# Group norms' statistics and coefficients kept in SBUF, with the openings of four stages rewritten

## The reference

```python
def _gn(v, G=32, eps=1e-5):
    B_, C_, H_, W_ = v.shape
    g = v.reshape(B_, G, C_ // G, H_, W_)
    m = jnp.mean(g, axis=(2, 3, 4), keepdims=True)
    s = jnp.var(g, axis=(2, 3, 4), keepdims=True)
    return ((g - m) / jnp.sqrt(s + eps)).reshape(v.shape)

x = x + _L0_conv_ref(_gn(x), ...)   # attention in a 5x5 window, 8 heads
x = x + _L1_conv_ref(_gn(x), ...)   # qkv, 5x5 depthwise + grouped 1x1, linear attention, projection
x = x + _L2_conv_ref(_gn(x), ...)   # per-channel softmax over a 7x7 window
x = x + _L3_conv_ref(_gn(x), ...)   # 3x3 convolution, its weights mixed per image from pooled _gn(x)
```

## Time and profile before

| | us |
|---|---|
| median of 3 runs | 7782.99 (7781.92 to 7786.57) |
| the profiled execution | 7781.12, span 7779.3 |
| PE busy | 7307.5 (94%) |
| DVE busy | 5660.4 (73%) |
| POOL busy | 4676.4 (60%) |
| ACT busy | 3664.9 (47%) |

### The profile page before, as it was taken

The page is one execution under the profiler, slowest core; times in us unless marked ns, Lnnn a source line. Parts: engine busy times, 40 slices in busy tenths (PEclk is TensorE's granted clock), DMA queues, the critical chain, the costliest instruction groups (busy, mean ns, idle before and its releaser), DMA issues. The chain is left out here.

```text
span 7779.3 us, 137220 instructions
## 1 busy us (share of the span) xinstructions
PE 7307.5 (94%) x53058; PEld 6275.6 (81%) x53058; DVE 5660.4 (73%) x8853; ACT 3664.9 (47%) x7040; POOL 4676.4 (60%) x2130
## 2 busy tenths in 40 slices
PE   5999998989998899699999999999999999997999
PEld 4777776879998777378888888888888888886999
DVE  5666666334443455499999999999999999996664
ACT  3565555423332333155555555555555555554322
POOL 3555553023333000189898899889898898895332
PEclk9999999999999999899999999999999999998999
DMA  3111112865555975122222222222222222214552
GB/s 140 66 62 59 59 62 73 298 179 147 148 145 144 259 210 167 58 53 59 64 51 51 64 63 53 55 60 53 60 63 59 49 57 65 60 41 117 151 161 78
DMA packets 651429, 751.13 MB, mean 97 GB/s; under 512 B 467573, under 2 KB 500469, under 8 KB 629222
## 3 DMA queue, kind: packets, MB, share of 16 engines
q1 hardware_dynamic: 581318, 483.44, 22.4%
q0 software_dynamic: 52288, 230.92, 12.1%
q10 hardware_dynamic: 17376, 30.54, 1.1%
HBM read 397.01 MB, written 193.76 MB: 76 GB/s over the span
## 5 line engine op out<-in xcount | busy, mean ns | idle before, releaser
L1960 POOL TENSOR_TENSOR e_ev<-e_se,e_v 128x1536 f32<-128x1536 f32 (+1 forms) x832 | 3073.9, 3822 | 242.5 <-ACT e_se L1891 242.0
L1891 ACT ACTIVATE e_se<-e_stage 128x512 f32<-128x512 f32 x2880 | 1714.7, 597 | 1517.2 <-PE e_stage L1707 1486.9
L2061 DVE SCALAR_TENSOR_TENSOR e_stage<-e_k,e_rl,e_qp 128x512 f32<-128x512 f32 x3136 | 2255.1, 745 | 223.7 <-ACT e_se L1891 184.6
L1714 PE MATMUL e_pv_sum<-e_ident,e_ev 128*128 128x128 f32 x12544 | 1821.9, 272 | 0.0
L1707 PE MATMUL e_stage<-e_top,e_minus 128*128 128x512 f32 x3136 | 1568.2, 502 | 101.3 <-DVE e_stage L2061 100.9
L1714 PEld LDWEIGHTS e_pv_sum<-e_ident,e_ev 128*128 128x128 f32 x12544 | 1480.9, 140 | 135.6 <-issue 85.2
L1714 PE MATMUL e_pe_sum<-e_ident,e_se 128*128 128x128 f32 x9472 | 1417.1, 272 | 12.8 <-ACT e_se L1891 12.8
L1714 PEld LDWEIGHTS e_pe_sum<-e_ident,e_se 128*128 128x128 f32 x9472 | 1173.6, 140 | 232.8 <-issue 40.1
L911 POOL DMA_DIRECT2D agg<-c_ot x384 | 334.9, 874 | 878.2 <-ACT c_ot L989 768.7
L403 POOL TENSOR_TENSOR a_pr<-a_pr,a_rden 128x480 f32<-128x480 f32 x512 | 495.0, 989 | 546.8 <-DVE a_rden L636 546.8
L1707 PEld LDWEIGHTS e_stage<-e_top,e_minus 128*128 128x128 f32 x3136 | 594.6, 190 | 233.3 <-DVE e_stage L2061 154.7
(11 more groups left out here) (180 smaller groups left out, 12371.1 us busy)
## 6 DMA issues: line engine op xcount, KB each, us to landing
e_acc<-e_se POOLq DMA_DIRECT2D x128, 1024.0 KB, 7.6
qkv<-b_ot SPq DMA_DIRECT2D x120, 512.0 KB, 5.9
c_xt<-qkv SPq DMA_DIRECT2D x384, 160.0 KB, 3.8
agg<-c_ot POOLq DMA_DIRECT2D x384, 160.0 KB, 2.5
f_ws<-in_L_w_sets SPq DMA_DIRECT2D x32, 1152.0 KB, 8.0
a_xb<-in_x SPq DMA_DIRECT2D x24, 768.0 KB, 5.0
a_xr<-in_x SPq DMA_DIRECT2D x32, 512.0 KB, 3.8
x<-a_xr SPq DMA_DIRECT2D x32, 512.0 KB, 2.7
```

Source lines behind the costliest of these rows:

```text
L1714: last = nc.tensor.matmul(total[:, c * PART:(c + 1) * PART], lhsT=src[:, c * PART:(c + 1) * PART], rhs=ident[:], is_transpose=True, start= ...
L1891: nc.scalar.activation(exps(t, j), stage[:, bank_of(t, j), :], ACT.Exp).then_inc(exp_done, 1)
L1960: nc.gpsimd.tensor_tensor(split(ev[(t * NG2 + g) % NEV][:, 0:size]), split(exps(t, o * K2 + i, size)), window(v[h], h, u, o, i, size), ALU ...
L2061: nc.vector.scalar_tensor_tensor(rows(stage[:, bank_of(t, j), :]), win, rl[:, h, o:o + 1], rows(qp[:]), ALU.add, ALU.mult).then_inc(multip ...
```

## The change

The statistics `st`, the coefficients `cf`, the pooled `mean` and the matrix `gm` become SBUF tiles of one object that lives through all blocks. The blocks `s_` and `n_` are gone: the chain of norm operations is the first thing that DVE, PE and ACT do inside the block that uses the norm, and nothing of it goes through DRAM. The measuring of the input is in `a_`, with three buffers in place of four, and the weights of `a_` are loaded between the maps. Then four openings are changed:

- `a_`: bands and masks of the first two bands are asked for while the maps are measured; from the third band on the coefficients are copied by a DMA from SBUF to SBUF.
- `c_`: only the first four groups' weights are loaded ahead of the first two groups of qkv, the rest behind them.
- `d_`: POOL's first two loads of the residual wait for the first turned tile.
- `e_`: the first band waits for its own tile to be cleared alone, the order of the clearing is changed, the upper edge of the first band isn't normalised and so needs no overwriting, the dummy products read weights and no longer x, and the first running extreme is opened ahead of the copies of V. For each band, statistics are written where they stay; the DMAs of coefficients and statistics are gone.
- `f_`: pairing the columns of the first two bands moves from DVE to POOL, the first weight set is asked for ahead of the first band, and ACT rounds the second band after the first weights.

The core of the diff:

```diff
-    norm_coefficients(nc, norm_sems, 2, stats[2], coef[2], w["group_mean"])
-    channel_attention(nc, norm_sems, xs[2], coef[2], xs[3], stats[3], ...)
+    channel_attention(nc, norm, xs[2], xs[3], w["L2_w_t"], w["L2_rel"], w["identity"], w["zeros"])
...
+    def product(self, pe, call, bank):
+        if call == 0:
+            pe.wait_ge(self.matrix_in, 16)
+        pe.wait_ge(self.averaged, call + 1)
+        self.nc.tensor.matmul(bank[:, 0:self.NS * 2], lhsT=self.gm[:], rhs=self.ms[:].rearrange("p n s -> p (n s)"),
+                              start=True, stop=True).then_inc(self.grouped, 1)
+    def root(self, act, call):
+        act.wait_ge(self.var_ready, call + 1)
+        self.nc.scalar.activation(self.std[:], self.var[:], ACT.Sqrt).then_inc(self.std_ready, 1)
+    def links(self, dve, call, bank, measured, pooled=False):
+        dve.wait_ge(self.measured, measured)
+        for i in range(self.NS):
+            h, b = divmod(i, B)
+            last = nc.vector.bn_aggr(ms[:, i, :], self.st[:, h, b])
...  (the chain that follows is that of L142 to L159)
 window_attention, sync
+            for k in range(0, NMAP, 2):
+                load_map(sp, k)
             sp.dma_start(wt[:], w_qkv_t.rearrange("(h p) o -> p h o", p=PART)).then_inc(consts_in, 16)
+            norm.load_matrix(sp)
...
+            for k in range(NMAP + NMAP % 2, B * HALVES, 2):
+                load_map(sp, k)
...
-                sp.dma_start(cf[u][:], coef[b]).then_inc(band_in[u], 16)
+                if g >= 2:
+                    sp.dma_start(cf[u][:], norm.cf[:, b]).then_inc(cf_in[u], 16)
 grouped_conv, sync
-            half = GROUPS // 2
-            for i in range(2):
-                sp.dma_start(band[:, i * half:(i + 1) * half], w_band[:, i * half:(i + 1) * half]).then_inc(consts_in, 16)
+            sp.dma_start(band[:, 0:EARLY], w_band[:, 0:EARLY]).then_inc(consts_in, 16)
             sp.wait_ge(border_zero, 2)
-            with sp.Fori(0, TURNS) as n:
+            load_groups(0)
+            half = (GROUPS - EARLY) // 2
+            for i in range(2):
+                part = slice(EARLY + i * half, EARLY + (i + 1) * half)
+                sp.dma_start(band[:, part], w_band[:, part]).then_inc(bands_in, 16)
+            with sp.Fori(1, TURNS) as n:
+                load_groups(n)
 linear_attention, gpsimd
+            pool.wait_ge(turned, 1)
             load(0)
 channel_attention
-            sp.wait_ge(cleared, CLEARED["e"])
+            sp.wait_ge(cleared, CLEARED["a"] + 1)
             load_band(0)
...
-            clear_edge(0)
...
-                nc.tensor.matmul(stage[:, i, :], lhsT=ident[:], rhs=xb[:, 0, 0:TPX], start=True, stop=True)\
+                nc.tensor.matmul(stage[:, i, :], lhsT=ident[:], rhs=wt[:, 0].rearrange("p h o -> p (h o)"), start=True, stop=True)\
...
+            normalise(0)
             act.wait_ge(cleared, CLEARED["e"])
-            normalise(0)
             for p in parts(0):
+                if p == "V0":
+                    open_extreme(0, OPENS[0])
                 copy_projection(0, p)
...
-            for x in (xb, *k, *v, near, pair):
+            for x in (xb, k[0], pair, near, v[0], k[1], v[1]):
 dynamic_conv, sync
+            load_set(0, 0)
             sp.wait_ge(cleared, CLEARED["f"])
             load_band(0)
-            for c in range(NWS):
+            for c in range(1, NWS):
 dynamic_conv, gpsimd
+            def pair_columns(u):
+                pool.wait_ge(normalised, (u + 1) * HALVES)
+                nc.gpsimd.tensor_tensor(to_pairs(u, 0, 2), of_columns(u, 0, 2), of_columns(u, 2, 2), ALU.subtract).then_inc(x_paired, 1)
+                nc.gpsimd.tensor_tensor(to_pairs(u, 2), of_columns(u, 1), of_columns(u, 2), ALU.add).then_inc(x_paired, 1)
+                nc.gpsimd.tensor_tensor(to_pairs(u, 3), of_columns(u, 2), of_columns(u, 1), ALU.subtract).then_inc(x_paired, 1)
+            pair_columns(0)
+            pool.wait_ge(paired, NPAIRED)
             for g in range(NG):
...
+                if g == 1:
+                    pair_columns(1)
                 pool.wait_ge(x_high_ready, g + 1)
 dynamic_conv, scalar
             round_x(0)
-            round_x(1)
             begin_mix(0, 1)
             round_w(0, 0)
+            round_x(1)
 dynamic_conv, vector
-            pair_columns(0)
-            mix(0, 0, 1)
-            pair_columns(1)
-            for k in range(2, K3):
+            for k in range(1, K3):
                 mix(0, 0, k)
```

More of the change, by code:

```diff
@@ L237, in window_attention @@
         consts_in = sem("consts_in")
-        cleared = sems["cleared"]
+        map_in = [sem(f"map_in{i}") for i in range(NMAP)]
+        cleared = norm.cleared
+        cf_in = [sem(f"cf_in{u}") for u in range(2)]
         normalised_x = sem("normalised_x")
@@ L554, in _ @@
         def _(act):
+            for k in range(1, B * HALVES, 2):
+                load_map(act, k)
             act.wait_ge(consts_in, 64)
@@ L623, in _, with measure_map @@
         def _(dve):
+            def measure_map(k):
+                b, h = divmod(k, HALVES)
+                dve.wait_ge(map_in[k % NMAP], (k // NMAP + 1) * 16)
+                for i in range(STATS):
+                    last = nc.vector.bn_stats(norm.st[:, h, b, i, :], xm[k % NMAP][:, i * NPX // STATS:(i + 1) * NPX // STATS])
+                last.then_inc(norm.measured, 1)
+            for k in range(B * HALVES):
+                measure_map(k)
+            norm.links(dve, 0, pj, MEASURED["a"])
             dve.wait_ge(consts_in, 64)
@@ L702, with qkv_project @@
 CROWS = CHUNK // WW
-def qkv_project(nc, x_in, coef, qkv, w_t):
+def qkv_project(nc, norm, x_in, qkv, w_t):
     ctx = ExitStack()
@@ L777, in _ @@
         def _(pe):
+            norm.product(pe, 1, pq[:, 0])
             pe.wait_ge(w_low_ready, 1)
@@ L1392, with channel_attention @@
 NG2 = K2 * len(ROW_PARTS)
[L1395 removed]
+def channel_attention(nc, norm, x_in, x_out, w_t, rel, ident_in, zeros):
     ctx = ExitStack()
@@ L1801, in _ @@
         def _(act):
+            norm.root(act, 2)
             act.wait_ge(consts_in, 80)
@@ L2146, with dynamic_conv @@
 COLUMN_ORDER = (0, 2, 1)
-def dynamic_conv(nc, sems, x_in, coef, pooled, x_out, w1_t, w2_t, b2, w_sets, ident_in):
+def dynamic_conv(nc, norm, x_in, x_out, w1_t, w2_t, b2, w_sets, ident_in):
     ctx = ExitStack()
```

317 lines of the change are left out of this document (134 added, 183 removed).

## The result

The changed kernel takes **7691.29 us** (median of 4 runs, 7678.91 to 7693.47), beside 7782.45 (7779.42 to 7786.57) for the kernel before on the same chip; ratio 0.9879, 95% interval 0.9862 to 0.9896. The forecast was 7696, 7682 to 7716. The profiled execution spans 7690.6 us: 88.7 less than before, where the sum of terms said 87.0.

The account below looks back on a forecast made before the run. PE was taken to bound the kernel, busy 94% of the span, with idle time to win in the openings. Terms summed to -87.0 us from 7781.1, giving 7694.1; the median's 1.9 more made 7696, range 7682 to 7716.

Parts of the forecast that it names:

- `a_`, term -16.1: Opening of `a_`: PE's first product comes 16.1 us earlier (13.4 to 17.3), with the last map 0.8 late.
- each map landing about 1 us before its turn, except the last: Measuring in `a_`: with three buffers every map but the last arrives about 1 us before DVE needs it.
- `f_`, first weights, -16.0: Opening of `f_`: the first turned weights on PE come 16.0 us earlier.
- DVE's first mix waits until about 7130, and all after it slips by 1.4: Opening of `f_`: POOL's pairing holds DVE's first mix until about 7130, making all after it 1.4 us later.
- `f_`, second weight, +0.5: Mixes of `f_`'s second weight: POOL's pairing and rest of band 1 meet DVE again, costing 0.5 us.
- Behind the first convolution, which has 13 us: `f_`, second weight: POOL's 11 to 13 us meeting DVE lie behind the first convolution's 13 us, so 0.5 is left.
- Rival 1: Blocked and shared: last map half-shared +2.7, PE cold in projections +1.7, POOL and DVE holding in `f_` +5.5; 7706, chance 0.17.
- Loops, 0: Loops: DMAs of coefficients and statistics go or become copies inside SBUF; nobody waited for them, so 0 us.
- `d_`, 0: Opening of `d_`: bound by bytes, so moving 1 MB to 10 us later gives 0 us (-3 to +2).
- gains given back: Gains of `c_` and `f_` lost to later weights, sets and bands by DMA; 7720 us, chance 0.05.
- copies in `a_`'s loop: SBUF copies of coefficients delay each of 30 bands in `a_`; with 5 us a band 7846 us, chance 0.03.
- old DMAs: A stage's chain could still wait for an old DMA; near no change, the rest of the chances, 0.01.

Follow-up runs that it names:

- kept_warm: Changed kernel with dummy PE products in `a_`, `c_`, `e_`, `a_`'s constants behind the maps, `d_`'s residual later, `f_`'s band 1 paired by DVE; 7693.29 us.
- other_orders: Changed kernel with `a_`'s maps split over two queues, two groups' weights ahead in `c_`, `e_` awaiting all clears, `f_`'s first set behind the band; 7696.30 us.
- parts_undone: Changed kernel with one part undone each: `c_` weights first, `d_` residual at once, `e_` extreme behind V, `f_` columns paired by DVE; 7708.81 us.
- all_openings: openings_further plus dummy PE products in `a_`, 11 of them as soon as the constants are there; 7668.05 us.
- before_padded: Kernel before with only an unused tile of 2272 bytes a partition ahead of all others; 7775.50 us.
- norms_alone: Changed kernel with the redrawn openings of `c_`, `d_`, `e_`, `f_` undone, except `e_`'s upper edge, dummy products and clearing order; 7717.53 us.
- before_cf_first: Kernel before with `cf` allocated ahead of all other tiles of `f_`, moving the weights by 64 bytes; 7772.01 us.
- changed_again: The changed kernel itself, unaltered, run again for a second trace of the same program; 7686.28 us.
- openings_further: Changed kernel with maps over both queues in `a_`, dummy products in `c_` and `e_`, `f_`'s first set behind the band and adds moved earlier; 7682.39 us.

## Why the prediction was right, step by step

The time was right (the forecast lay 4.7 us above the median), and the mechanisms of `b_`, `c_` and `e_` hold with their sizes: -10.2 for -10.5, -8.4 for -9.0, -29.8 for -31.0 (the band flew 8.8 us where I took 7.6), -3.6 to -6.7 by the pairs of traces for -4.9 inside `e_`. But the sum hides errors of both signs, and that they cancel is luck.

- **`a_`, term -16.1:** -10.5 to -15.4 by the pairs of traces, -12.7 by the means; 1.0 of the difference is in the base, since the trace that the forecast was worked out from has 81.2 where the mean of three is 80.2. The failing step is "each map landing about 1 us before its turn, except the last": DVE waited 1.34 us for the sixth map in one trace and 2.09, 1.29 and 1.07 for three maps in the other, and the first came at 14.5. Maps that fly side by side are what makes it late: with the constants behind the maps it still came at 14.1 (kept_warm), with one map after the other at 9.7 (other_orders). What kept single maps back is not shown.
- **`f_`, first weights, -16.0:** -17.4. The step "DVE's first mix waits until about 7130, and all after it slips by 1.4" failed: POOL's three pairings took 4.8 us, not 5.6 and more, and were over at 7059.57, when DVE's first mix became free to start anyway (7059.41). Hold: 0.14 us for my 1.4.
- **`f_`, second weight, +0.5:** +4.0. "Behind the first convolution, which has 13 us" was the wrong cover: the first adds are queued on DVE behind these mixes, and PE waits for them. parts_undone sets the pairing's whole worth at 0.7 to 1.5 us. Rival 1 named this mechanism and put 5.5 on it. Its other two parts didn't come in the first trace; in the second, the first projection of `a_` was 4.1 behind the forecast's 65.1, by late maps, and the opening of `e_` 1.3 longer than forecast, by the clock.
- **Loops, 0:** `f_` is 6 us shorter, by where its tiles stand, which no part of the argument looked at; `e_` 1.0 to 2.9, cause not sought.
- **`d_`, 0:** neither confirmed nor refuted. By the means the opening is 1 us shorter, but the rate of its DMAs moves it by up to 8 with nothing changed, more than the edit could.

By the means of the table, the gain is 3.4 us smaller in `a_`, 2.1 in the opening of `f_`, 2.1 over `b_`, `c_` and `e_`, and 8 larger in the loops of `e_` and `f_`. The loop of `e_` stayed within 5 us; by more than 4, my bound for a wrong forecast, only the openings of `a_` and `d_` were off, both in the second trace alone. By that sign the forecast would have failed on the second trace. The remaining rivals (gains given back, copies in `a_`'s loop, old DMAs) found nothing in any trace.

## What to carry to other kernels

Where stages stand end to end, one kernel can carry one edit in each, and the milestones of its trace part them; but take a second trace of the same kernel first, since here a stage bound by DMA moved by 8 us and one that PE opens at the lower clock level by 3, with nothing changed. When work goes to another engine to free a busy one, follow both queues to the next thing that PE waits for: here 4.1 of the 4.8 us gained at the first weights of `f_` were paid back 26 us later. Send what is needed first through both queues, in pieces, in the order of use.

## What the runs showed of the hardware

- A product of 256 columns took 116.1 to 118.6 ns at the same granted clock, by the distance of its two operands in SBUF (80704, 80800, 80768, 80736 bytes, from fast to slow).
- In the changed kernel the column of the granted clock reads 1.00 from 65.8 to 83.5, yet a product of 480 columns takes 0.60 there and 0.38 later, and products start 0.40 and 0.22 apart; 480 columns in 0.40 us are 1.2 GHz, the lower of the two levels. The column is no evidence there: the trace's first record of the clock is a rise at 82.9, and without a record the column shows 1.00. In all_openings the records begin at 51.3, and the column agrees with the 0.60 us:

```profile
61.50:64.90 3.40, 3.20 (x8) 2.51 (x8) 0.00 (x0) 1.26 (x2) 3.40 (x3) 0.51 0.57 185
```

- The first rise of the clock dates the scatter of `a_`: where it comes 17.0 to 17.6 us behind the first projection (before_padded, changed, parts_undone, norms_alone), the first output comes 42.1 behind; where it comes 25.4 to 27.0 behind (before, before_cf_first, changed_again, other_orders, openings_further), 44.8 to 45.4.
- DVE's operations with two SBUF tiles are held also where they are tiny: 1.25 us for 0.17 (other_orders), 6.38 for 0.96 (before_cf_first); eight `bn_aggr` beside the same POOL instruction took their usual 1.98.
